# A fused transformer stack on one core: state sums two half steps later, scan loads one half step earlier, scans 136 half steps apart, and a new spread of the other stages

## What is computed

```python
x = x + _L0_attn_ref(_layernorm(x))   # pre-norm block: windowed attention (16 heads of 16, window 128), then an MLP 256-1024-256 with gelu
x = x + _L0_ffn_ref(_layernorm(x))    # token shift, r = sigmoid(xr Wr), k = relu(xk Wk)^2, r * (k Wv)
x = x + _L1_attn_ref(_layernorm(x))   # in_proj, convolution of 4 taps, silu, delta = softplus(.), then the state scan below
x = x + _L1_ffn_ref(_layernorm(x))    # one of 8 experts (256-1024-256, relu), picked per sequence by the mean over its rows

dA = jnp.exp(delta[..., None] * A)                     # 512 channels x 16 states
BX = delta[..., None] * Bm[:, :, None, :] * xc[..., None]
_, hs = jax.lax.associative_scan(comb, (dA, BX), axis=1)
y = jnp.einsum('blen,bln->ble', hs, Cm) + D * xc
```

## Time and profile before

| | us |
|---|---|
| median of 3 runs | 3627.49 |
| runs | 3621.44, 3627.49, 10848.22 |
| profiled execution, device time | 3620.18 |
| its span in the trace | 3618.1 |
| PE busy | 3042.8 (84%) |
| POOL busy | 2786.8 (77%) |
| DVE busy | 2583.2 (71%) |
| ACT busy | 2415.5 (67%) |
| DMA queue, share of 16 engines | 72.3% |

### The profile page before, as it was taken

How to read it: one execution, slowest core, us unless ns; L and a number is a source line. 1 busy time by engine, 2 the same in 40 slices (tenths; PEclk the granted TensorE clock), 3 DMA queues, 4 the chain that set the end, 5 groups by cost and what they waited for, 6 DMA issues and landing times.

```text
span 3618.1 us, 58031 instructions
## 1 busy us (share of the span) xinstructions
PE 3042.8 (84%) x17392; PEld 1885.8 (52%) x17392; DVE 2583.2 (71%) x5920; ACT 2415.5 (67%) x5331; POOL 2786.8 (77%) x2583
## 2 busy tenths in 40 slices
PE   5888888897988979899898989889898998987557
PEld 3555454464655646465464646556464654644236
DVE  3356878687787868778686876878687776878870
ACT  4577767676776857677685767768576776855431
POOL 1117989898887979888897988889798888977880
PEclk9998898899999989999898989989898998988678
DMA  2017877877777877877777887778878778789981
GB/s 73 7 42 192 214 208 193 225 215 238 207 204 222 217 229 216 241 209 204 223 218 228 220 237 210 207 222 226 230 215 234 210 204 231 213 248 256 284 235 37
DMA packets 423337, 736.59 MB, mean 204 GB/s; under 512 B 53427, under 2 KB 100147, under 8 KB 423027
## 3 DMA queue, kind: packets, MB, share of 16 engines
q1 hardware_dynamic: 423026, 732.89, 72.3%
HBM read 648.84 MB, written 83.89 MB: 203 GB/s over the span
## 4 chain that ended last, share of the span: by engine, by line
PE 60%; ACT 9%; POOL 9%; DVE 9%; issue 6%; DMA 5%; SPq 2%; ACTq 0%; DVEq 0%; POOLq 0%
PE bank L466 16%; PE bank L474 9%; PE bank L589 6%; PE bank L499 6%; PE bank L736 5%; PE bank L722 5%; PE bank L511 5%; POOL u_rows L1506 4%; PE bank L670 4%; DMA u_rows<-u_dram 3%; PE bank L527 3%; POOL u_rows L1499 3%; DVE u_rows L1287 3%; ACT prob L791 2%; DMA d_rows<-delta_dram 1%
## 5 line engine op out<-in xcount | busy, mean ns | idle before, releaser
L1506 POOL TENSOR_TENSOR u_rows<-u_rows,c_rows 128x512 f32<-128x512 f32 x1024 | 1304.8, 1277 | 169.3 <-DVE state L1292 116.4
L1499 POOL TENSOR_TENSOR u_rows<-u_rows,b_rows 128x512 f32<-128x512 f32 x960 | 1225.8, 1278 | 71.8 <-DMA u_rows<-u_dram 70.8
L962 ACT ACTIVATE bank<-d_rows,a_rep 128x512 f32<-128x512 f32 x1024 | 697.7, 688 | 296.5 <-DMA d_rows<-delta_dram 150.6
L1287 DVE TENSOR_TENSOR_SCAN u_rows<-bank,state,u_rows 128x512 f32<-128x512 f32 x512 | 644.0, 1271 | 83.3 <-ACT bank L962 78.9
L1287 DVE TENSOR_TENSOR_SCAN u_rows<-bank,u_rows 128x512 f32<-128x512 f32 x512 | 622.8, 1216 | 85.0 <-ACT bank L962 81.2
L791 ACT ACTIVATE prob<-prob,neg_max 128x256 f32<-128x256 f32 x1024 | 509.9, 505 | 42.9 <-DVE neg_max L1074 42.7
L670 PE MATMUL bank<-u_rows,sum_n 128*32 128x512 f32 x2048 | 309.1, 679 | 237.9 <-POOL u_rows L1506 235.0
L1074 DVE CUSTOM_DVE_ANT_0 prob<-bank,band 128x256 f32<-128x256 f32 x896 | 337.6, 416 | 178.0 <-PE bank L499 159.8
L511 PE MATMUL bank<-ident,prob 128*128 128x128 f32 x2048 | 330.3, 290 | 89.0 <-ACT prob L791 70.8
L511 PEld LDWEIGHTS bank<-ident,prob 128*128 128x128 f32 x2048 | 247.0, 148 | 230.8 <-issue 185.1
L499 PE MATMUL bank<-kT,q_own 32*128 32x256 f32 x2048 | 299.9, 412 | 47.4 <-DVE neg_max L1074 25.1
(11 more groups left out here) (167 smaller groups left out, 5276.4 us busy)
## 6 DMA issues: line engine op xcount, KB each, us to landing
u_rows<-u_dram SPq DMA_DIRECT2D x1024, 256.0 KB, 5.4
d_rows<-delta_dram SPq DMA_DIRECT2D x1024, 256.0 KB, 5.1
w<-in_W SPq DMA_DIRECT2D x28, 1024.0 KB, 7.2
zs_dram<-region_b SPq DMA_DIRECT2D x64, 256.0 KB, 2.8
xc_dram<-region_b SPq DMA_DIRECT2D x64, 256.0 KB, 2.5
u_dram<-region_b SPq DMA_DIRECT2D x64, 256.0 KB, 3.4
delta_dram<-region_b SPq DMA_DIRECT2D x64, 256.0 KB, 3.1
yg<-xc_dram SPq DMA_DIRECT2D x64, 256.0 KB, 4.9
```

The lines of the kernel that those rows point to most:

```text
L962: e.activation(banks[at.bank][:, :], delta_of(i, k), ACT.Exp, scale=a_rep[:, j:j + 1]).then_inc(filled[at.bank], 1)
L1287: e.tensor_tensor_scan(rows, banks[at.bank][:, :], rows, state[:, k:k + 1] if i % 2 else 0.0, ALU.mult, ALU.add).then_inc(drained[at.bank], 1)
L1499: e.tensor_tensor(rows, rows, b_rows[:, :], ALU.mult).then_inc(bx_ready.sem, 1)
L1506: e.tensor_tensor(rows, rows, c_rows[:, :], ALU.mult).then_inc(hc_ready.sem, 1)
```

## The change

Six numbers of the offsets and periods, the cost lists, and the times of four threads:

```diff
-SCAN0, LOAD_AT, INPUT_AT, DECAY_AT, KEEP_AT, OUT_AT, SUM_AT, GATE_AT = 10, -9, -4, -2, 1, 3, 6, 8
+SCAN0, LOAD_AT, INPUT_AT, DECAY_AT, KEEP_AT, OUT_AT, SUM_AT, GATE_AT = 10, -10, -4, -2, 1, 2, 8, 10
-SCAN_PERIOD = 133
+SCAN_PERIOD = 136
-    (("scan",), 2, 0.05, 0.05 + SCAN_STEPS / SCAN_PERIOD),
+    (("scan",), 2, 0.041, 0.041 + SCAN_STEPS / SCAN_PERIOD),
     (("back",), 3, 0.16, 0.35),
-    (("route",), 3, 0.36, 0.39),
-    (("fetch",), 4, 0.39, 0.40),
-    (("expert",), 4, 0.44, 0.97),
+    (("route",), 3, 0.407, 0.437),
+    (("fetch",), 4, 0.437, 0.447),
+    (("expert",), 4, 0.467, 0.979),
```

More of the change, by code:

```diff
@@ L43 @@
 TILES = 64
-SCAN0, LOAD_AT, INPUT_AT, DECAY_AT, KEEP_AT, OUT_AT, SUM_AT, GATE_AT = 10, -9, -4, -2, 1, 3, 6, 8
+SCAN0, LOAD_AT, INPUT_AT, DECAY_AT, KEEP_AT, OUT_AT, SUM_AT, GATE_AT = 10, -10, -4, -2, 1, 2, 8, 10
 GATE_LOAD_AT = 14
 SCAN_STEPS = SCAN0 + 2 * (TILES - 1) + GATE_AT + 1
-SCAN_PERIOD = 133
+SCAN_PERIOD = 136
 COSTS = {
[L50 to L54, removed]
+    "head": [2.45] * 6,
+    "attention": [1.81] * 2 + [0.8] * (ATT0 - 2 + 18) + [1] * 54 + [1.5] + [1.57] * 4,
+    "mlp": [1.5] * 2 + [1] * 8 + [1.31] * 8 + [4] + [1.04] * 8 + [2.5] * 3,
+    "rwkv": [1.5] * 5 + [1] * 11 + [1.6] + [2.5] * 3,
+    "middle": [1.68] * 2 + [1] * 8 + [1.15] * 8 + [1] * 11,
     "scan": [1] * SCAN_STEPS,
-    "back": [1.5, 1, 1, 1, 1, 1.5, 1.5, 1.5, 1, 1],
+    "back": [2.26] + [1] * 4 + [2.06] * 3 + [1] * 2,
     "route": [1] * 3,
     "fetch": [1],
-    "expert": [1] * 25,
+    "expert": [1] * 12 + [0.95] * 13,
 }
@@ L119, in schedule @@
         for i in range(2 * batches):
-            spent = 0.0
+            chain, spent = [], 0.0
             for stage in stages:
[L122 to L127, removed]
+                if stage == "route" and i % 2 == 0:
+                    continue
+                which = i // 2 if stage == "route" else i
                 for step, cost in enumerate(COSTS[stage]):
-                    at.append((i + lag + begin + (end - begin) * spent / total, thread, stage, which, step))
+                    chain.append((i + lag + begin + (end - begin) * spent / total, thread, stage, which, step))
                     spent += cost
-    return [(stage, which, step) for _, _, stage, which, step in sorted(at, key=lambda s: s[:2])]
-class Use:
-    def __init__(self, bank, n, f):
-        self.bank, self.n, self.f = bank, n, f
-def banks_of(order, batches):
+            if chain:
+                chains[thread, i] = chain
     begins, ends = {}, {}
@@ L149, in banks_of, with earlier @@
                 ends.setdefault((stage, shared, last), []).append(name)
[L150 to L153, removed]
+    def earlier(thread, i):
+        out = [] if THREADS[thread][0] == ("scan",) else [(thread, i - 1)]
+        if thread:
+            out.append((thread - 1, i | 1 if THREADS[thread][0] == ("fetch",) else i))
+        return out
+    order, uses = [], {}
+    idle, counted, signalled = list(range(8)), [0] * 8, [0] * 8
+    while chains:
+        for key, chain in sorted(chains.items(), key=lambda c: c[1][0][:2]):
+            _, _, stage, i, step = chain[0]
+            shared = stage == "scan" and shared_inputs(i, batches)
+            names = begins.get((stage, shared, step), ())
+            if len(names) <= len(idle) and not any(c in chains for c in earlier(*key)):
+                break
+        else:
+            raise AssertionError("no bank is idle")
+        order.append((stage, i, step))
+        for name in names:
             bank = idle.pop(0)
@@ L159, in banks_of @@
             idle.append(uses[stage, i, name].bank)
-    return uses
+        del chain[0]
+        if not chain:
+            del chains[key]
+    return order, uses
 def build_block_stack(nc, d):
@@ L185, in build_block_stack @@
     assert WINDOW == P and SEQ % G == 0 and HD == 16 and GROUPS == 2 and ED // EL == TILES and KE * 16 == TILES
-    order = schedule(BATCH)
-    uses = banks_of(order, BATCH)
+    order, uses = schedule(BATCH)
     with ExitStack() as ctx:
```

5 lines of the change are left out of this document (4 added, 1 removed).

## The result

| | before | changed |
|---|---|---|
| median of the runs | 3627.53 us | 3583.28 us |
| nearest runs | from 3621.44 | 3576.54 to 3587.42 |
| span of the profiled execution | 3618.1 us | 3574.4 us |
| ratio of the times, 95% interval | | 0.990, 0.987 to 0.993 |

The change makes the kernel 1.0% faster by the recorded ratio (the two medians alone would give 1.2%, inside of its interval), where I had forecast 2.7%. The ratio leaves out the one execution of before that took 10848 us. The time lies inside of the range and the direction is right, but less than half of the gain came. The lines of the functions are 16 higher in the changed kernel (line 1440 is 1456).

The account below looks back on a forecast made before the run. PE's loop was taken as the bound: 181 us nearly all busy, then 30.3 us from V (line 1440's start) to the mlp. Terms of -6.5 us over 13 periods (-85) and draining -5 gave 3530 us; range 3445 to 3645.

Parts of the forecast that it names:

- What bounds the kernel: PE's loop sets the period: 181 us from mlp to next V (line 1440's start), then 30.3 us to the mlp.
- Term 1: From V (line 1440's start) to the mlp: begins 4.0 us sooner, -3.1 us a period after 0.9 moved ahead of V.
- a sign of being wrong: ACT still waiting 3 us for the delta row behind V would mean the stores were not its cause.
- The reload goes out at about the same time after V: Reload of the mlp's weights stands behind three more tiles, but tiles run three ahead; part of the items costed 0.
- The same work in other places of a PE that is full there: Banks, route, fetch, expert and cost lists: 0 us a period, bounds -2 and +2.
- Term 2: The last probabilities get about 4 us longer to be made, so PE waits less: -2.9 us a period.
- nearly nothing: Rival, chance 0.30: PE's full part of 181 us counts, other small waits fill the freed places; 3588 us.
- Term 3: The sum in mid scan no longer waits some 2.13 us: -2.0 us a period, bounds 0 and -2.7.
- Term 4: Ring of u rows: later sums cut load margins from 8.0 to 4.9 us; +1.5 us a period, bounds 0 and +8.
- Filling: The kernel's start, before the steady periods: forecast to change by 0.
- the slower rival: Chance 0.10: u row landings cost POOL 1.5 us at each of 16 loads, +7 us a period, 3710 us.
- the rival of the larger gain: Chance 0.20: DVE has less ahead of the statistics, PE's clock stays up; -10 to -12 us a period, 3470 us.

Follow-up runs that it names:

- e3: Changed kernel with layer norm's two tensor_scalar moved from DVE to POOL and a semaphore for each reload of the mlp's weights; 0.972, 3514.41 us.
- e10: Changed kernel with spacing 133, the scan's begin and the places of before, so new offsets and cost lists alone; 0.974, 3524 us.
- e8: The changed kernel run again as it is, on another chip; 0.9885, 3575.9 us.
- e5: Kernel before with only the scan's new offsets; cost lists, spacing, scan's begin and places of before; 1.031.
- e4: Changed kernel with the scan's offsets of before; lists, spacing and places stay new; 0.998, 3602 us.
- e11: The change without its new offsets and places: new lists, spacing 136 and scan's begin, against the kernel before; 0.994, 3599 us.
- e9: Changed kernel with the cost lists of before; offsets, spacing, scan's begin and places stay new; 1.035, 3746 us.
- e2: Changed kernel with a semaphore for each of the two reloads of the mlp's weights, nothing moved; 0.988, 3569.8 us.
- e1: Changed kernel with layer norm's two tensor_scalar moved from DVE to POOL; 0.981, 3548.5 us.
- e6: Changed kernel with route, fetch and expert at their places of before, all else new; 0.981, 3549 us.
- e14: New offsets and lists, other settings of before, but head's and attention's cost lists also those of before; 0.990, 3582.5 us.
- e15: New offsets and lists, other settings of before, but the cost lists of mlp, rwkv and middle also those of before; 0.987, 3566.8 us.
- e7: Kernel before with layer norm's two tensor_scalar moved from DVE to POOL and a semaphore for each reload of the mlp's weights; 1.006.

## Why the prediction was right in part and wrong in size

- **What bounds the kernel: right for before, not enough for the changed kernel.** PE's waits do set the time: where their sum fell (e3: 57 us less in twelve periods than in the changed kernel, e10: 39 us less), the time fell with it. But they are not only behind V. The stretch from V to the mlp is nearly as short in the changed kernel (26.9 us) as in e10 (26.4), and their periods are 209.9 and 205.0 us. For the rest of the period, from the mlp to the next V, my terms came to -2.5 us (+0.9 - 2.9 - 2.0 + 1.5); it got 1.9 us longer (1.2 in e8). (The 211.4 us that I took for a period are 211.05 by the two rows of line 1440; nothing hangs on it.)
- **Term 1, V to the mlp, -4.0 us: right in kind, 3.0 measured** (29.9 to 26.9 on average). The sum's wait went from 9.01 to 1.11 us, `zb` is waited for 9.12 us at V+22.7 where I had V+22.8, and the sum runs at the higher clock. The reason that I gave for `nb` holds too: ACT's wait for a delta row ahead of it went from 3.4 us a period to nothing. ACT still waits 2.7 us for a delta row at V+27 to V+29, near the 3 us that I had named as a sign of being wrong, but that row comes behind `nb` and is not in the mlp's way. No one part of the change does this alone: ahead of `nb` ACT waits 3.5 us with the offsets alone (e5), 2.9 with all but the offsets (e4), 0.6 with lists and spacing (e11) and 0.0 with all but the lists (e9).
- **"The reload goes out at about the same time after V", 0 us: the first step that failed.** Its time was right (V+15.8 against V+15.6), the conclusion was not. I moved its consumer 4 us forward in term 1 and did not ask what else that consumer waits for. PE waits 34.5 us for it in twelve periods. Taking that wait away gave nothing that the runs can tell by itself (e2) and 0.9% where DVE was free too (e3 against e1); with intervals of some 0.5% that it counts only together with the other is likely, not shown.
- **"The same work in other places of a PE that is full there", 0 us: the step that failed most.** It was argued from PE's busy time. But the order is also that of POOL and DVE. The new order put POOL's work so that DVE was held for 5 to 7 us, and PE waited 51.7 us. Spacing and places cost 1.5% (e10 0.974, the changed kernel 0.9885), 4 to 5 us a period where my bound was 2: 0.8% by the places (e6), the rest by the spacing and the scan's begin, for which I had no term at all. The lists, costed at 0 too, are worth 5.9% beside the new offsets (the order from which I read terms 1 to 3 had them in it): without them the mlp begins later than before (e5 by 0.6 us, e9 by 4.8), and the rest of the period grows by 7.8 and 5.6 us.
- **Term 2, -2.9: the 2.65 us wait is gone, its worth is not.** PE's waits for probabilities rose from 46.7 to 56.3 us: others, 2.91 us some 100 us behind V and 1.42 us some 160 us behind it, came in its place. This was the mechanism of the rival "nearly nothing", and it held for this term. **Term 3, -2.0:** PE's waits for POOL before the sums in mid scan (1.7 to 3.2 us in each period before) are gone, and the 13.4 us that are left stand behind V, so it was right. In e4, with the old offsets, 0.55 us of it is left, so that the scan runs ahead does most of this.
- **Term 4, the ring, +1.5:** POOL's waits for u rows rose from 46.6 to 112.3 us from 490 to 3190 us, 5 us a period more, as the margins said. No wait of PE's for POOL rose by as much; in e10 POOL waits 88.4 us there at a period of 205.0. POOL's wait before line 1456 fell from 105.8 to 57.1 us meanwhile, so I read it as taken out of POOL's slack; what it cost was not tested by itself. The larger bound and the slower rival fell.
- **Filling, 0:** it gave 22.9 us. It is in every kernel with new lists (fourth V at 620 to 635 us) and in none with the old lists and POOL's work as it was (648 to 650); e14 and e15 keep it with either half of them. About 5 of the 22.9 us lie before the first V (109.3 to 104.2 us), where e8 with the same kernel has 109.3 again, so some 17 us are the change's. 11 of these lie between the third and the fourth V (202.6 to 191.5 us). From the second V to the fourth, PE of the kernel before waits 18.3 us for POOL's "out" and 8.2 us for `zb`; in the changed kernel less than 1 us for "out" is left there, and 17.2 us for `zb` and 16.8 us for a step of the scan stand in its place. What gave the 11 us stays open.
- **The rivals.** The time is that of "nearly nothing" (3588), but not by its reason in the main: PE's full part gave way as soon as the two new waits were gone. The change took back what my forecast had won, in places that I had priced at 0: -6.5 us a period forecast, -1.1 to -1.9 measured, -5.8 with e3's edits, and -6.0 in e10, where spacing and places are left out. That -6.0 comes so near to -6.5 is in part luck. Of it, 3.4 us are less waiting ((304.3 - 263.7) / 12) and 2.6 us are less busy time of PE ((2227.2 - 2196.2) / 12) at a higher mean clock (0.95 against 0.93), which stood in no term but in the rival of the larger gain; and e10's waits for probabilities rose to 67.5 us, against term 2. In e3 4.9 of the 5.8 us are waiting.

## What to carry to other kernels

When a step is brought forward, list everything that it waits for, and find which of these is next: the gain ends there. When a table moves work, look at every engine that it orders, not just at the one that is full; a small instruction on one engine can be held by a stream on another, and this profile showed it as a long busy time of the held instruction, not as a wait. And offsets, spacing and places in a period are one setting: the same edit was worth -1.4%, -1% and +3.1% beside three settings of the rest, so none has a price of its own. Compare a total with its terms, too: two of them can be wrong and the sum come out.

## What the runs showed of the hardware

- DVE's `tensor_scalar` of 128 x 4 elements, 0.17 us by itself, took up to 7.1 us while POOL ran without a gap. In e6 one got in at the end of the POOL instruction that was running, after 1.07 us, though the next one followed at once; in the changed kernel one let five pass. What decides between the two stays open. The two of e6, DVE (first fence) and POOL:

```profile
2016.06 1.07 DVE L1060 TENSOR_SCALAR rstd_b<-mean_var_b 128x4 f32<-128x4 f32 x1
```

```profile
2015.83 1.28 POOL L1515 TENSOR_TENSOR u_rows<-u_rows,b_rows 128x512 f32<-128x512 f32 x1
2017.06 1.27 POOL L1522 TENSOR_TENSOR u_rows<-u_rows,c_rows 128x512 f32<-128x512 f32 x1
```

- The same work on POOL (two instructions more in each layer norm) made the changed kernel 0.8% faster (e1) and, with e2's edit, the kernel before 0.6% slower (e7). In the first DVE was held by POOL, in the second PE waited for POOL's "out".
- A wait of PE can cost more than its length, by the clock behind it. Twelve periods of e5 have 83 us more of PE's busy time than e10's for the same matrix work (2279.2 against 2196.2 us, at a mean granted clock of 0.92 against 0.95), nearly as much as the difference in its waiting (352.6 against 263.7 us). e5's row, beside e10's above:

```profile
648.18:3280.00 2631.82, 2279.21 (x13029) 1402.44 (x13028) 1904.19 (x4374) 1803.63 (x3997) 2143.25 (x1974) 0.92 0.75 211
```
